# Reordering the first loads of a fused attention and FFN kernel, and lending a piece of w2 the rows of attention

## What is computed

```python
def block(x, ctx):
    # cross attention over one batch group: n_q = 128, mask keeps j % 128 == i
    h = layernorm(x)
    kv = ctx @ Wkv; v = second half of kv          # with 154 context rows and that mask
    out = softmax(masked q k^T) @ v @ Wout + bout   # one or two context rows per query row
    x = x + out
    # FFN with 8-bit activations and ternary weights
    h = layernorm(layernorm(x)) * gamma + beta
    xq, sx = act_quant(h)                           # per row: 127 / max|h|, round, clip
    wq, sw = weight_quant(w1)                       # per tensor: 1 / mean|w|, round, clip to -1..1
    h = gelu((xq @ wq.T) / (sx * sw) + b1)
    out = the same with w2 and b2
    return x + out
```

## Time and profile before

| what | value |
|---|---|
| median of three runs | 541.06 us |
| the profiled execution's own time | 543.86 us |
| its span in the profile | 542.0 us |
| mean granted TensorE clock | 0.993 of full |
| PE, DVE, ACT, POOL busy | 96%, 83%, 81%, 75% |

### The profile page before, as it was taken

How to read it: one execution, slowest core, us unless ns; L and a number is a source line. 1 busy time by engine, 2 the same in 40 slices (tenths; PEclk the granted TensorE clock), 3 DMA queues, 4 the chain that set the end, 5 groups by cost and what they waited for, 6 DMA issues and landing times.

```text
span 542.0 us, 8082 instructions
## 1 busy us (share of the span) xinstructions
PE 521.8 (96%) x2387; PEld 226.6 (42%) x2434; DVE 452.4 (83%) x758; ACT 436.8 (81%) x444; POOL 408.4 (75%) x533
## 2 busy tenths in 40 slices
PE   6999789799999999999999999999999999999997
PEld 3443334344444444444444444444444444444443
DVE  1799998999998888888888888889888889877653
ACT  1478988878888888888888888888888888887762
POOL 2099796988998888888898888888888889863300
PEclk8999999999999999999999999999999999999999
DMA  7996834486555545555665446556555554534433
GB/s 271 400 343 217 221 76 106 131 205 161 141 141 142 122 124 120 129 132 138 142 139 125 123 121 142 141 109 138 118 131 132 138 142 103 103 70 98 102 77 97
DMA packets 137014, 78.72 MB, mean 145 GB/s; under 512 B 114245, under 2 KB 114309, under 8 KB 136971
## 3 DMA queue, kind: packets, MB, share of 16 engines
q1 hardware_dynamic: 135819, 76.12, 55.4%
q10 hardware_dynamic: 1152, 2.10, 1.1%
HBM read 33.88 MB, written 17.05 MB: 94 GB/s over the span
## 4 chain that ended last, share of the span: by engine, by line
PE 77%; DVE 3%; issue 2%; ACT 1%; DMA 1%; DVEq 0%; ACTq 0%
PE py L1049 37%; PE p L1034 36%; PE p L1024 3%; DVE hmax L811 1%; DMA hT<-hq 1%; DVE hx L788 1%; DVE hid L805 0%; ACT hid L574 0%; ACT hq L583 0%; DVE xr L834 0%; DVE stat L780 0%; DVE xmax L793 0%; ACT hqT L592 0%; DVE hqT L825 0%; DVE hstep L814 0%
## 5 line engine op out<-in xcount | busy, mean ns | idle before, releaser
L1034 PE MATMUL p<-w1q,xqT 128*128 128x512 bf16 x995 | 229.1, 380 | 3.7 <-issue 1.6
L1049 PE MATMUL py<-w2q,hqT 128*128 128x512 bf16 x1006 | 229.9, 379 | 1.9 <-DVE hqT L825 1.0
L574 ACT ACTIVATE hid<-p,xdeq 128x1024 f32<-128x1024 f32 x128 | 141.8, 1108 | 27.1 <-PE p L1034 17.5
L583 ACT ACTIVATE hq<-hid,hscale 128x2048 int8<-128x2048 f32 x64 | 128.1, 2002 | 42.9 <-DVE hscale L817 42.9
L1049 PEld LDWEIGHTS py<-w2q,hqT 128*128 128x128 bf16 x1024 | 100.1, 98 | 122.1 <-DVE hqT L825 1.5
L1034 PEld LDWEIGHTS p<-w1q,xqT 128*128 128x128 bf16 x1024 | 94.8, 98 | 122.1 <-issue 14.3
L385 POOL TENSOR_TENSOR xr<-xr,attn 128x512 f32<-128x512 f32 x64 | 83.3, 1321 | 19.1 <-DVE attn L723 19.1
L811 DVE TENSOR_REDUCE hmax<-hid 128x1 f32<-128x1025 f32 x64 | 78.1, 1220 | 21.1 <-ACT hid L574 20.7
L400 POOL TENSOR_TENSOR hx<-hx,beta_b 128x512 f32<-128x512 f32 x64 | 91.9, 1456 | 2.0 <-ACT hx L559 2.0
L404 POOL TENSOR_TENSOR xr<-xr,b_b 128x512 f32<-128x512 f32 x64 | 93.0, 1474 | 0.0
L805 DVE TENSOR_REDUCE hid<-hid 128x1 f32<-128x1024 f32 x64 | 77.4, 1210 | 8.9 <-ACT hid L574 8.9
(11 more groups left out here) (86 smaller groups left out, 293.1 us busy)
## 6 DMA issues: line engine op xcount, KB each, us to landing
xr<-x SPq DMA_DIRECT2D x64, 256.0 KB, 2.9
out<-xr SPq DMA_DIRECT2D x64, 256.0 KB, 2.4
raw<-w1T SPq DMA_DIRECT2D x8, 512.0 KB, 11.3
wout<-wout_d ACTq DMA_DIRECT2D x8, 256.0 KB, 8.2
hid<-wvT SPq DMA_DIRECT2D x8, 256.0 KB, 10.0
wout<-w2T SPq DMA_DIRECT2D x3, 512.0 KB, 8.2
xr<-w2T SPq DMA_DIRECT2D x2, 512.0 KB, 6.4
attn<-ctxm_d SPq DMA_DIRECT2D x4, 256.0 KB, 8.5
```

What stands on the lines that cost most here:

```text
L574: nc.scalar.activation(hid[:, t % 2, h * HALF:(h + 1) * HALF], p1[:, h * HALF:(h + 1) * HALF], ACT.Gelu, scale=col(xdeq, t)).then_inc(gelu ...
L583: nc.scalar.activation(hq8[:, t % 2, :], hid[:, t % 2, 0:HID], ACT.Copy, scale=col(hscale, t))\
L1034: mm = nc.tensor.matmul(p1[:, n * D:(n + 1) * D], xT[:, k, :], w1q[:, k, n * D:(n + 1) * D], start=False, stop=(k == KD - 1))
L1049: mm = nc.tensor.matmul(py[:, t % 2, :], hqT[:, t % 2, c // 2, c % 2, :], w2q[:, c, :], start=(c == 0), stop=(c == 2 * NJ - 1))
```

## The change

It has three parts.

1. The two loads of batch 0's context (`ctx_rows`, `ctx_end`) go from the head of SP's queue to the head of ACT's, so that Wv's chunks come second on SP, behind b1 alone. gamma goes from ahead of the chunks to behind x tile 1.
2. The rest of SP's list up to the first transposition is reordered: x tiles 3 to 6 each stand later among w1's and w2's pieces, and five pieces of w2 (0 to 4) stand ahead of `transpose_x(0)` instead of two.
3. Piece 5 of w2 lies in `attn[:, 0:2]` instead of in `wout[:, 0:2]`; pieces 6 and 7 move down to `wout[:, 0:4]`. Since `attn[:, 0]` is written by `attn_rows(3)`, this step now also waits for six roundings of w2.

```diff
-        w2raw += [hqT_words[0], xr[:, 14:16, :], hqT_words[1]] + [wout[:, 2 * a:2 * a + 2, :] for a in range(3)]
+        w2raw += [hqT_words[0], xr[:, 14:16, :], hqT_words[1], attn[:, 0:2, :], wout[:, 0:2, :], wout[:, 2:4, :]]
...
-                if j == 5:
+                if j == 6:
                     sp.wait_ge(wvo_done, KD)
...
-            load_ctx_b0()
             load_b1()
-            sp.dma_start(gamma_b[:, :], gamma.partition_broadcast(P)).then_inc(gamma_loaded, 16)
             load_wv(0)
...
             load_x(0)
             load_w1(0)
-            load_w1(1)
             sp.dma_start(bout_b[:, :], bout.partition_broadcast(P)).then_inc(bout_loaded, 16)
             load_x(1)
-            load_x(2)
+            sp.dma_start(gamma_b[:, :], gamma.partition_broadcast(P)).then_inc(gamma_loaded, 16)
+            load_w1(1)
             load_w1(2)
             load_w1(3)
+            load_x(2)
             store_b1()
-            load_x(3)
-            sp.dma_start(beta_b[:, :], beta.partition_broadcast(P)).then_inc(beta_loaded, 16)
             load_w1(4)
             load_w1(5)
-            load_x(4)
-            load_x(5)
-            load_x(6)
+            sp.dma_start(beta_b[:, :], beta.partition_broadcast(P)).then_inc(beta_loaded, 16)
+            load_x(3)
             load_w1(6)
             load_w1(7)
+            load_x(4)
+            load_w2(0)
             load_b1_rows()
-            load_w2(0)
+            load_x(5)
+            load_w2(1)
             load_ctx()
-            load_w2(1)
-            transpose_x(0)
             load_w2(2)
+            load_x(6)
             load_w2(3)
             load_w2(4)
+            transpose_x(0)
             load_w2(5)
...
         def _(act):
+            act.dma_start(ctx_rows, ctx_b0[0:P, :]).then_inc(ctx_b0_loaded, 16)
+            act.dma_start(ctx_end, ctx_b0[P:KV, :]).then_inc(ctx_b0_loaded, 16)
             for m in range(KI):
...
             def attn_rows(i):
                 dve.wait_ge(attn_done, i + 1)
+                if i == 3:
+                    dve.wait_ge(wround_act[1], 6)
```

More of the change, by code:

```diff
@@ L208, in load_w2 @@
                     .then_inc(w2_loaded[j], 16)
-            def load_ctx_b0():
-                sp.dma_start(ctx_rows, ctx_b0[0:P, :]).then_inc(ctx_b0_loaded, 16)
-                sp.dma_start(ctx_end, ctx_b0[P:KV, :]).then_inc(ctx_b0_loaded, 16)
             def load_ctx():
```

## The result

The changed kernel takes 546.53 us (median of 4 runs, 546.37 to 546.72), beside 541.13 us for the kernel before on the same chip (540.9 to 542.37). By these medians it is slower by 5.4 us. The ratio is 1.0081, with a 95% interval of 1.0056 to 1.0106, which is 4.4 us, between 3.0 and 5.7. The forecast was 544.9 beside 541.06, that is +3.8 us, in a range from 542.2 to 546.8.

The account below looks back on a forecast made before the run. PE alone bounds the kernel from 117 us, engines waiting on each other before. PE's second layer 3.4 us late plus 2.0 for the clock, less 1.6 coming back, gives +3.8 on 541.06: 544.9 us, range 542.2 to 546.8.

Parts of the forecast that it names:

- The start: Loads up to `bias(1)`: Wv's chunks land earlier, x tile 3 limits POOL to 1.4 us; PE and ACT lead 2.2 us.
- the rival of a smaller start: Start: lead of only 1.0 us and no quicker `centre(8)`, giving +5.6, 546.7 us; chance 0.07.
- The rival that the slow DMA stretch belongs to what is moved away: DMA from 3 to 9 us: the hole goes, lead 4.4 us, end 542.7 us; chance 0.10.
- The wait: At `attn_rows(3)`: DVE stands until ACT's sixth rounding at 79.6 us; PE's second layer starts 3.4 us later, at 88.1.
- The clock: PE's second layer: after 5.4 us idle, 4 us at half rate, costing +2.0 us.
- a held clock: Behind PE's idle stretch: clock stays full, DVE's 3.0 us decide, end 0.7 us lower at 544.1; chance 0.12.
- What comes back: Behind the second layer's start: PE's idle 1.00, 0.2 and 0.4 us take up 1.6 of 5.4 us, leaving +3.8.
- 6.0 less the lead: Whole kernel, the sum in short: the end moves by 6.0 us less the lead at 61 us.

Follow-up runs that it names:

- e6: Kernel before with only batch 0's two context loads moved to the head of ACT's queue; 538.85 us, ratio 0.9942.
- e12: Kernel before with 16 more unused products of ones on PE behind the context mean; 540.06 us, ratio 0.9962.
- e0: Kernel before, unchanged, timed and profiled once more; 542.17 us, ratio 1.0002, its profiled execution 541.21 us.
- e2: Kernel before with part 3 alone (w2's piece 5 in attention's rows, and the wait); 549.76 us, ratio 1.0137.
- e1: Changed kernel without part 3, so the new order of loads alone; 539.26 us, ratio 0.9954.
- e4: Changed kernel with 18 more unused products on PE between the fifth first layer and the second layer; 543.85 us, ratio 1.003.
- the first profile: Profiled execution of the unchanged kernel before, which the prediction was made from; 543.86 us.
- e3: Changed kernel with ACT's sixth rounding of w2 moved right behind the fifth, ahead of `gelu(2, 0)`; 538.51 us, ratio 0.9937.
- e9: Changed kernel with `attn_rows(3)` moved behind the sixth clip of w2 in DVE's list; 538.78 us, ratio 0.9943.
- e8: e3 with x tile 3 asked for right behind tile 2, ahead of w1's pieces 4 and 5; 537.94 us, ratio 0.9922.
- e10: e8 with three more products of ones on PE ahead of the mean row; 537.77 us, ratio 0.9916.
- e11: e6 with w2's pieces 2, 3 and 4 asked for ahead of the first transposition; 539.73 us, ratio 0.9947.

## Why the prediction was right, and where its sum was off

The direction, the place and the mechanism were right: a wait put into DVE's list behind an ACT instruction that itself waits for PE. Measured are +5.4 us by the four-run medians and +4.4 (3.0 to 5.7) by the ratio, forecast were +3.8. That the total came out so near is in part luck, for its terms were off in opposite directions. Point by point:

- *The start.* The first product moved from 11.17 to 7.92 us, and x tile 3 became the limit, as worked out: it landed at 29.4 where 29.9 was forecast. The lead at `bias(1)` was 2.55 us against 2.2, the time 58.49 against 58.9. ACT's wait for w2 went. Chunk 3, which DVE's mean row hangs on, came earlier than worked out: 11.92 us against 12.8; of this lead of 3.3 us 2.6 reached POOL, for the clock fell in PE's pause before the mean row. The prediction had named that under the rival of a smaller start; it cost some 0.5 us. Where the prediction was short is the source. The rival that the slow DMA stretch belongs to what is moved away was given 0.10, and it isn't settled: from 3 to 9 us the rate rose from 266 to 335 GB/s in the kernel after and to 304 in e6, but e12, with the queues of before, moved 310 (e0 282, e2 277). e6 also shows that the two context transfers alone gain as much as the whole order, and that the rest adds nothing to it that the runs can tell (539.26 for e1, 538.85 for e6). In the traces w2's earlier pieces take ACT's wait away, and x tile 3 and the later first transposition make new ones; that these cancel is a reading. The Trainium skill says that transfers issued by different engines share the same 16 DMA engines, so that issuing from several of them saves only the time of the issue ("DMA: Bandwidth & Descriptors", Issuing engines are not separate DMA queues). Here moving 0.32 MB from SP's queue to ACT's (e6) had SP issue Wv's first chunk only 0.83 us earlier than in e0, but brought the first product 2.9 us forward and made the kernel 3.4 us faster, so the measurement decides; how much of it is order, rate or clock isn't taken apart.
- *The wait.* ACT's sixth rounding ended at 79.3 us (forecast 79.6), DVE stood for 7.06 us (6.6), and `centre(8)` took 0.73 us (0.75). Behind the copy a second group was quicker that I had not counted: the six clips took 2.08 us, and 2.70 before. So the second layer started at 87.12, not 88.1. From `bias(1)` on the price is 28.63 - 23.68 = 4.95 us, where the prediction had 3.4 + 2.2 = 5.6.
- *The clock.* It fell to 0.50 behind 4.78 us of idling, for some 3.3 us. Forecast were 2.0 us; the products lost 1.70, and the end 2.46 (the kernel after against e4). The Trainium skill's rule that the throttled clock is what PE falls back to without activity ("TensorE: Matmul & The Clock Gate", Part 1) agrees in this stretch: with the gap filled the clock stayed at 1.00. The prediction's remark that the trace differs from the rule at the very start is not borne out. The granted clock is shown as 1.00 there, but the warming products of the first 5 us took 421 to 444 ns each and their loads of weights 328 to 333, as loads of the same shape do at 0.50 (329), so they ran at the slow level; e12's filling products, of the same shape, took 275 to 290 and their loads 192. And the prediction's 0.7 us for a held clock should be 0.8 (3.8 less 3.0).
- *What comes back: the term that was mis-sized.* The prediction let PE's idle 1.00, 0.2 and 0.4 us behind the second layer take 1.6 us of the delay up. Against the first profile some did come back: the part up to `bias(8)` grew only by 33.03 - 32.46 = 0.57 us, although the products lost 1.70, since DVE's wait of 1.05 us for the late transposition is gone. That is 1.1 us and not 1.6, and with the wait's smaller price the forecast for a profiled execution, 547.7 us, was too high by 1 us. But I then set the same difference of +3.8 on the median, 541.06. An execution like e0's, 541.21 us, has no such slack (30.39), and against it nothing comes back: part by part -2.07 at the start, +4.94 for the wait, +2.64 for the clock with the slow centrings, -0.01 for the rest, which is +5.5 us, the difference of these two executions. The median of the kernel before lies between the two kinds (542.1 us in 26 executions), and so does the 4.4 us of the ratio.
- *The sum as the prediction put it in short*, "6.0 less the lead": the 6.0 holds against an execution like the first profile (5.8 in e2) and is too small against one like e0. There the third part costs 7.4 us (e2) to 8.0 us (after less e3), 4.94 and 2.64 by the table. Term by term against e0: the wait cost 4.94 and not 5.6, the clock 2.64 and not 2.0, the lead was 2.07 and not 2.2, and nothing of the 1.6 came back. That DVE holds the chain from 91.6 to 112 us, on which the prediction leaned, also belongs to the first execution: in e0 DVE is as full there (19.88 of 20.40 us), and has 0% of the chain.

What stays open: why the transposition of `widen_h(2)` is late by 1 us in some executions (the first profile, e1, e9) and not in others (e0, e3, e6, e8, e10, e11). It comes with and without the change. With the slow centrings beside it, it accounts for 2.07 us of the kernel's spread of 4.7 (in the first two groups), and what the rest is the runs don't tell.

## What to carry to other kernels

A buffer that is lent costs a wait at the place where its owner comes back; look at what the releasing instruction is queued behind, and not only at how early its data arrive. If it can go ahead of a group that waits for another engine, or the copy behind the work that others wait for, the lending is free as far as these runs can tell (e3 and e9: 8 us for one moved line).

Slack that one profile shows may belong to that execution. Before it is counted as cover, look at whether it comes from a transfer or a wait that varies, and set off a sum from the median only with terms that the median execution has.

A gap on PE is paid twice, once as time and once as clock, and the second part can reach the end larger than the slower products alone show: 2.5 us here for 1.70, and with the full clock two steps on another engine were 1.0 us shorter as well.

## What the runs showed of the hardware

- The clock fell at gaps of quite different length, and held at gaps of the same length. Ahead of `bias(1)` PE did the same 12 products in 2.76 us and then waited 1.76 us in e6 and 1.80 in the kernel before: in e6 the clock fell right behind it, before it held. Ahead of the mean row PE waited 1.94 us in the kernel after and had 0.50 from 23 to 26 us; in e3 it waited 1.95 and kept 1.00. Ahead of its first product it waited 1.10 us in e3 and kept 1.00 from 8 to 10 us; in e10 it waited 1.23 and had 0.50.
- VectorE's same group of operations has two durations: two centrings 3.41 or 2.42 us, six clips 2.70 or 2.08, one centring 1.45 or 0.73. The longer clips and the longer single centring lie beside work of POOL, which is slower there too: its two products `hdeq<-hstep,wmean` took 0.70 us beside the slow clips of e3 and 0.33 us in the kernel after, where DVE stood still. Beside the two centrings POOL worked in both cases. An experiment with POOL kept away wasn't made.
- Behind `bias(8)` thirteen profiled executions of twelve programs take 424.7 to 425.3 us, so whatever happens ahead of it can be read off one time stamp.
